# First attention of a four-layer stack: where a step's first row-maximum unit stands in TensorE's order

## The reference, cut to what matters

```
q = x @ Wq + bq;  k = ctx @ Wk + bk;  v = ctx @ Wv + bv
scores = einsum(q, k) / sqrt(8) + mask        # per sequence: 8 x 4 x 56 rows of 1500
out = softmax(scores) @ v
x = layernorm(out @ Wo + bo + x)
```

## Time and profile before

| | us |
|---|---|
| median of 3 runs | 3276.99 |
| profiled execution, whole time | 3270.37 |
| profiled execution, span first to last instruction | 3268.5 |
| first attention's steady bodies (about 47 to 50 us each) | from about 145 to 1640 |
| TensorE busy over the span | 2863.0 (88%) |
| VectorE busy over the span | 2012.5 (62%) |
| ScalarE busy over the span | 1415.9 (43%) |

### The profile page before, as it was taken

How to read it: one execution, slowest core, us unless ns; L and a number is a source line. 1 busy time by engine, 2 the same in 40 slices (tenths; PEclk the granted TensorE clock), 3 DMA queues, 4 the chain that set the end, 5 groups by cost and what they waited for, 6 DMA issues and landing times. The chain is left out here.

```text
span 3268.5 us, 63507 instructions
## 1 busy us (share of the span) xinstructions
PE 2863.0 (88%) x18753; PEld 1515.8 (46%) x18753; DVE 2012.5 (62%) x4195; ACT 1415.9 (43%) x3023; POOL 661.8 (20%) x483
## 2 busy tenths in 40 slices
PE   5799999999999999999867888699999997888885
PEld 3344444444444444444334444356666664544443
DVE  3667677676767767677447887344454440168775
ACT  2255555555555555565622221254544443212221
POOL 5221221121122122112023333000000001033331
PEclk8699999999999999999978999799999998999997
DMA  6333333432433343243010000111111100100000
GB/s 198 106 83 114 108 112 85 121 108 76 120 108 105 91 121 108 75 121 102 16 63 1 1 1 1 47 34 28 33 32 29 32 17 30 60 1 6 6 1 12
DMA packets 117235, 205.18 MB, mean 63 GB/s; under 512 B 39765, under 2 KB 84546, under 8 KB 116546
## 3 DMA queue, kind: packets, MB, share of 16 engines
q1 hardware_dynamic: 116930, 201.08, 21.5%
HBM read 156.09 MB, written 44.59 MB: 61 GB/s over the span
## 5 line engine op out<-in xcount | busy, mean ns | idle before, releaser
L586 DVE CUSTOM_DVE_ANT_0 masked<-ps_a,mask 112x750 f32<-112x750 f32 x1024 | 941.7, 936 | 377.8 <-PE ps_a L473 369.1
L546 ACT ACTIVATE probs<-ps_a 128x448 f32<-128x448 f32 (+1 forms) x1536 | 743.3, 542 | 546.6 <-PE ps_a L439 542.8
L473 PE MATMUL ps_a<-ks,q_row 96*112 96x375 bf16 x2048 | 530.1, 342 | 58.0 <-DVE part_max L586 35.6
L439 PE MATMUL ps_a<-q_sc,ks 99*128 99x448 bf16 (+1 forms) x1536 | 450.5, 359 | 50.0 <-ACT probs L546 28.5
L459 PE MATMUL ps_a<-probs,vp 128*32 128x224 f32 x6144 | 378.4, 364 | 1.2 <-ACT probs L546 0.9
L473 PEld LDWEIGHTS ps_a<-ks,q_row 96*112 96x112 bf16 x2048 | 220.6, 133 | 329.8 <-issue 271.0
L2024 DVE CUSTOM_DVE_ANT_0 f_masked<-ps_c,f_mp 112x432 f32<-112x432 f32 x256 | 145.6, 605 | 221.3 <-PE ps_c L1876 218.7
L439 PEld LDWEIGHTS ps_a<-q_sc,ks 99*128 99x128 bf16 (+1 forms) x1536 | 132.5, 100 | 281.3 <-issue 232.5
L236 POOL CAST k_piece<-kv_t 64x1500 bf16<-64x1500 f32 x32 | 45.6, 1426 | 1042.8 <-ACT kv_t L228 1042.6
L459 PEld LDWEIGHTS ps_a<-probs,vp 128*32 128x32 f32 x6144 | 164.3, 111 | 160.0 <-ACT probs L546 60.8
L215 PE MATMUL ps_a<-ctx_t,wkv 128*128 128x375 f32 x512 | 198.6, 514 | 21.0 <-DVE x_nat L347 10.8
(11 more groups left out here) (283 smaller groups left out, 3978.3 us busy)
## 6 DMA issues: line engine op xcount, KB each, us to landing
ctx_t<-in_ctx_t SPq DMA_DIRECT2D x32, 1500.0 KB, 8.8
ks<-k_scr SPq DMA_DIRECT2D x64, 562.5 KB, 5.1
mask<-in_mask SPq DMA_DIRECT2D x64, 328.1 KB, 5.4
k_scr<-k_piece SPq DMA_DIRECT2D x64, 281.2 KB, 6.5
k_scr<-k_piece SPq DMA_DIRECT2D x64, 187.5 KB, 6.8
f_context<-in_ctx_t SPq DMA_DIRECT2D x32, 375.0 KB, 3.1
k_scr<-k_piece SPq DMA_DIRECT2D x64, 93.8 KB, 7.1
q_row<-q_scr SPq DMA_DIRECT2D x64, 84.0 KB, 4.5
```

The source lines that it names most:

```text
L439: mm = pe.matmul(out, ks[par][:, j, at], q_sc[par][:, j], start=True, stop=not with_mask)
L473: mm = pe.matmul(ps[0:2 * L, bank + i, 0:SC], q_row[which][:, j, h, gp * 2 * L:(gp + 1) * 2 * L], ks[which][0:SROWS, j, at], start=True, s ...
L546: act.activation(probs[t % 2][0:n, i], ps[0:n, k % SCORE_BANKS, 0:PW] .rearrange("p (h n) -> p h n", h=2), ACT.Exp).then_inc(probs_done, 1)
L586: dve.tensor_tensor_reduce(out=masked[:, u % 2], in0=two_banks(bank, 2 * L), in1=in_two(mask[which][:, c * SU:(c + 1) * SU]), scale=1.0, s ...
```

## The change

It moves each step's first row unit. In the list it gets a new place -1, and in step 9 it comes ahead of `neg` rather than behind it; so in that step the two change their bank pairs, and VectorE takes the row unit ahead of `neg`. On TensorE place -1 is issued ahead of the first pair of scores in every step. No instruction is added or removed on any engine.

```diff
     for t in range(NT):
         off, rows = (2, early) if t >= 9 else (1, late)
         mine = [("row", off, next(rows)) for _ in range(ROWS_AT[t])]
+        units.append((t, -1) + mine[0])
         if t == NEG_STEP:
             units.append((t, 0, "neg", 1, 0))
-        units.append((t, 0) + mine[0])
         if t in OTHERS_AT:
...
             for t in range(NT):
+                front(t, -1)
                 if cur:
                     scores(t, 0)
                 front(t, 0)
```

## The result

The changed kernel takes 3418.81 us, the median of 4 runs (3416.93 to 3428.81), against 3274.34 us for the kernel before in the same sessions (4 runs): ratio 1.0452, 95% interval 1.0427 to 1.0477. It is 144.5 us slower; 3414 with 137 us had been forecast. The profiled executions are 150.1 us apart (3420.51 and 3270.37).

What follows compares the result with a forecast made beforehand. It took the cycle from R1 over VectorE's reading to R0, PV and the next R1 as the bound. Loop bodies 120 us, full written-out bodies 15 and body 30 2 make 137 us more: 3414 us, range 3345 to 3470.

Steps and rivals of the forecast that it cites:

- step 9: Step with `neg`: row unit and scores can go at once behind the K and V products; gain 0.3 us.
- steps 1, 2, 5, 7, 8 and 10: Loop-body steps whose first row unit waits for VectorE's reading: first score pair leaves that wait, 0.65 us more each.
- Step 3: Loop-body step where VectorE's reading ends 0.15 us earlier relative to need: 0.50 us more.
- 4, 6 and 11: Loop-body steps released by ScalarE's reading of K and V products, with 0.35 us slack: 0.30 us more each.
- step 0: Body's first step, where loading the mask's flag holds the first unit in either order: taken as 0.
- written-out body: Body outside the loop: 2.5 us more, from 6 x 0.40 + 0.25 + 3 x 0.05 - 0.30.
- bound steps: Six of twelve steps whose first row unit waits for VectorE: 0.65 us more in loop bodies, 0.40 in written-out ones.
- the bodies outside the loop: Six full written-out bodies make 15 us, body 30 makes 2, bodies -2, -1 and 31 make 0.
- S0's lateness behind a held unit: First score pair starts 0.53 us behind a held row unit in loop bodies, 0.42 in written-out ones, 0.33 if unheld.
- The first (queue work hidden): Rival: scores enter the cycle but their queue work is hidden; 0.38 us a step, 71 us, 3348 us; chance 0.17.
- The clock: Rival: longer waits bring one clock fall per loop body, 72 us on top, 3486 us; chance 0.10.
- R0 held by S0: Rival: scores, not the bank, held the first row unit; 46 us less, 3231 us; not slower has chance 0.05.

Runs made afterwards that it cites:

- half-of-the-steps pair: Row unit moved only in steps 1, 2, 5, 7, 8, 10, or only in the others, against the kernel before: ratios 1.0306 and 1.0103.
- short reading: VectorE reads only 64 of each bank's 375 columns of a row unit: kernel before 3182.17 us, changed kernel 3270.85 us.

## Why the prediction was right

**What bounds a step** was read rightly: the cycle from R1 over VectorE to R0, PV and R1, which S0 filled. The half-of-the-steps pair and the short reading show it, and the signature is the forecast one: R0 0.12 behind VectorE's end, S0 at 0.53, PV at 1.06 behind R0 (1.08 predicted), three-row cycle 3.76 (3.6 to 3.9), waits for VectorE 152 us (100 or more).

**The steps of a loop body** (first line of the table by steps): steps 1, 2, 5, 7, 8 and 10 grew by 0.59 to 0.68 us, a mean of 0.63; 0.65 was predicted. Step 3 grew by 0.61 (0.50 predicted), 4, 6 and 11 by 0.38, 0.28 and 0.35 (0.30), step 0 by 0.13 (0), and step 9 gained 0.12 (0.3). Four loop bodies in a row take 211.8 us where they took 191.1, 5.2 a body; 5.0 was the sum. The body around a lap's end grew by 4.5, the others by 5.4: step 0 of a lap's first body, put at 0, gains 0.86. So the terms that were too low and this gain cancel in part, and the sum came out closer than its terms.

**The term that was mis-sized** is the written-out body: 2.5 us predicted, about 4.5 measured (49.6, 49.9 and 50.0 us from `neg` to `neg` against 45.2, 45.2 and 45.5; the last two grow by 2.9 and 2.3). I carried the 0.35 us of slack of steps 4, 6 and 11 over from loop bodies. In a written-out body S0 follows R2 by 0.42 and R0 follows S0 by 0.38, so R0 comes 0.80 behind R2, and ScalarE's release comes 0.73 behind it: the slack is 0.07, and each of the three steps pays 0.41 to 0.46 in place of 0.05. The bound steps pay 0.45 there, where 0.40 was predicted, and step 3 0.45, where it was 0.25. From `neg` to `neg` the 23 intervals between loop bodies grew by 119 us together and the eight others by 32, which is the 150 us between the profiled executions; by the sum the bodies outside the loop were to give 17.

**Why the price was right.** I put S0's lateness behind a held unit down to the branch and the scores' own waits, which the queue has still to go through. The table of the queue's instructions shows just that: behind the wait for R0's banks stand the branch, the register operation and S0's wait, one behind the other, 0.53 us from R0 to S0. Without the branch it is 0.34, and 0.32 with it where R0 wasn't held. The waits are separate instructions, as I had given as a reason against the first rival, though each is one of 51 ns in the trace, not two. The Trainium skill, "Advanced Engine Details and Errata" (Control Flow Timing), gives about 108 ns for a compare-and-branch. This trace does not agree: on TensorE's queue its records are 200 ns or longer, with a median of 221, and the measurement decides.

**The rivals.** The first (queue work hidden) gave 71 us; without the branch the change costs 89, and its price of 0.38 us a step is what the steps of that kernel show. So it describes that kernel, nearly, and not this one. The clock did not fall: 0.98 as before. R0 held by S0 is refuted: R0 did not start before VectorE's end, with S0 out of the way.

## What to carry to other kernels

An instruction in front of a wait that sets the pace is free as long as it fits into the wait (the branch in the six bound steps of the kernel before), and the same instruction behind it is paid: before reordering a queue, find for each step which release comes last, and move into that wait rather than out of it. To shorten such a cycle, issue sooner the producer whose reading is awaited (here R1), not the consumer that awaits it (here R0). That helps a step only until something else bounds it, as step 3 showed. A branch of the queue belongs where the queue has work in hand, not behind an instruction that stands at a wait.

## What was not expected of the hardware

A branch costs nothing that can be seen behind products that run freely (0.32 to 0.33 us from R0 or R2 to S0, which is the products' own time). Behind a unit that is held it costs 0.19 us in a loop body and 0.08 in a written-out one. In a loop body 0.11 of the 0.19 is thus the register operation that stands behind the branch; without the branch this operation is hidden. It is paid even if the unit is held for some 0.1 us only (in the changed kernel with the short reading S0 is 0.62 behind R0; 0.09 of that is a gap in the queue ahead of S0's wait that the trace does not explain). And half a group of value products with a row unit between the halves cost, in the step looked at, 0.23 us more than the two whole: 1.49 against 1.26.
